# Context features projected first, expert products turned, and a routing load in eight parts

## The reference, cut to what matters

```python
# layer 0: autocorrelation attention of x with ctx, then experts
logits = x @ gate_w.T; probs = softmax(logits); vals, idx = top_k(probs, 2)   # two of 16 experts a row
w = zeros.at[rows, idx].set(vals / sum(vals))
h = silu((x @ g.T).reshape(bs, 16, 112)) * (x @ u.T).reshape(bs, 16, 112)
out = einsum('bei,hei,be->bh', h, d_r, w)
# layer 1: cross attention of the layer-normed x (text) with ctx (features)
Q = einsum('btx,dx->btd', text, Wq) + bq
K = einsum('bpx,dx->bpd', features, Wk) + bk
attn = softmax(einsum('btd,bpd->btp', Q, K) / sqrt(1024))
attended = einsum('btp,bpd->btd', attn, features)
# then x = x + tanh(g) * (...) after each part, and the quantised feed-forward
```

## Time and profile before

| | us |
|---|---|
| median of 3 runs | 1470.27 (1467.56 to 1472.78) |
| the profiled execution | 1470.33 |
| span of its trace, first to last instruction | 1468.6 |
| TensorE busy | 1265.6 (86%) |
| VectorE, ScalarE, GpSimd busy | 761.1, 549.1, 629.8 |
| mean granted TensorE clock | 0.949 of full |

### The profile page before, as it was taken

The page is one execution under the profiler, slowest core; times in us unless marked ns, Lnnn a source line. Parts: engine busy times, 40 slices in busy tenths (PEclk is TensorE's granted clock), DMA queues, the critical chain, the costliest instruction groups (busy, mean ns, idle before and its releaser), DMA issues. The chain is left out here.

```text
span 1468.6 us, 20091 instructions
## 1 busy us (share of the span) xinstructions
PE 1265.6 (86%) x5843; PEld 851.6 (58%) x5849; DVE 761.1 (52%) x1981; ACT 549.1 (37%) x936; POOL 629.8 (43%) x990
## 2 busy tenths in 40 slices
PE   3899999999966899899999994499999999838876
PEld 1444545454526844357776772388888888624443
DVE  2878888888753460013333333544345432138995
ACT  2544444444305200024444444132222222148884
POOL 4767777776540007112122123742333210047885
PEclk9999999999978599999999997699999999979999
DMA  5212124102005303127778855363233221121111
GB/s 186 87 58 63 51 84 164 38 15 101 1 0 199 149 11 103 29 69 262 257 229 257 264 194 186 88 157 115 87 114 100 89 68 34 53 65 44 57 49 80
DMA packets 53669, 156.28 MB, mean 106 GB/s; under 512 B 7152, under 2 KB 17392, under 8 KB 53488
## 3 DMA queue, kind: packets, MB, share of 16 engines
q1 hardware_dynamic: 39328, 113.65, 22.1%
q0 software_dynamic: 14288, 41.97, 10.1%
HBM read 113.09 MB, written 45.66 MB: 108 GB/s over the span
## 5 line engine op out<-in xcount | busy, mean ns | idle before, releaser
L44 PE MATMUL xa_bank<-xa_xT_hi,M_hi 128*128 128x256 f32 x512 | 154.0, 301 | 0.0
L46 PE MATMUL xa_bank<-xa_xT_hi,M_lo 128*128 128x256 f32 x512 | 145.0, 283 | 0.0
L45 PE MATMUL xa_bank<-xa_xT_lo,M_hi 128*128 128x256 f32 x512 | 144.8, 283 | 0.0
L52 PE MATMUL la_bank<-la_osum,la_tab 128*128 128x512 f32 x256 | 121.0, 617 | 15.9 <-POOL la_osum L297 14.7
L1132 PEld LDWEIGHTS ex_bank<-ex_gu,ex_xT 128*128 128x128 f32 x624 | 116.8, 190 | 21.1 <-issue 20.0
L1132 PE MATMUL ex_bank<-ex_gu,ex_xT 128*128 128x224 f32 x624 | 124.9, 353 | 0.8 <-ACT ex_xT L1057 0.8
L297 POOL TENSOR_TENSOR la_osum<-la_oprod 128x512 f32<-128x512 f32 x64 | 80.1, 1273 | 96.2 <-DVE la_oprod L476 96.2
L1325 ACT ACTIVATE xa_A<-xa_bank,shift 128x256 f32<-128x256 f32 x64 | 30.4, 475 | 210.2 <-PE xa_bank L46 210.2
L1020 POOL TENSOR_TENSOR ex_current<-ex_listed,ex_nought 128x1 int32<-128x1 int32 x42 | 8.0, 190 | 229.8 <-DVE Wq L1090 226.8
L44 PEld LDWEIGHTS xa_bank<-xa_xT_hi,M_hi 128*128 128x128 f32 x512 | 98.2, 192 | 2.8 <-issue 1.7
L45 PEld LDWEIGHTS xa_bank<-xa_xT_lo,M_hi 128*128 128x128 f32 x512 | 98.0, 191 | 2.5 <-issue 1.7
(11 more groups left out here) (274 smaller groups left out, 2872.9 us busy)
## 6 DMA issues: line engine op xcount, KB each, us to landing
produced<-Wq SPq DMA_DIRECT2D x39, 512.0 KB
ex_gu<-in_gate_up SPq DMA_DIRECT2D x16, 896.0 KB, 6.6
X<-in_x SPq DMA_DIRECT2D x8, 1024.0 KB, 7.5
la_v_raw<-in_ctx SPq DMA_DIRECT2D x16, 512.0 KB
produced<-la_zeros SPq DMA_DIRECT2D x16, 512.0 KB, 5.1
normal<-rt_xn SPq DMA_DIRECT2D x16, 512.0 KB, 3.6
xa_fT<-in_ctx_T SPq DMA_DIRECT2D x8, 1024.0 KB, 5.5
xa_f<-in_ctx SPq DMA_DIRECT2D x8, 1024.0 KB, 5.6
```

The lines of the kernel that those rows point to most:

```text
L44: pe.matmul(out, a[0], b[0], start=first, stop=False)
L45: pe.matmul(out, a[0], b[1], start=False, stop=False)
L46: return pe.matmul(out, a[1], b[0], start=False, stop=last)
L52: return pe.matmul(out, a, b, start=first, stop=last)
```

## The change

In `route` and before it: the last batch's mean and deviation are made at the start of `route` instead of at the end of `lag_attention`; the weight that is loaded early is Wq, and the second, Wk, is loaded in eight parts of 512 KB, one ahead of the loop and one after every second store. In `experts`: gate and up weights are the stationary operands and the turned rows move, 128 wide, so that both products come out turned; the transpose of `hid` and the copy `hT` are gone. In `context_attention`: M is applied to the context features (`g_block`) instead of to the text. The features are split in hi and lo, and turned text `xT` is a plain float32 copy. Scores of a batch come in one piece at its end. `M_lo` is made partly on VectorE. All batches are written out.

```diff
 lag_attention (pool; the vector engine alike)
-                if before2 and before2[2] == 1:
+                if before2 and before2[2] == 1 and not (isinstance(before2[1], int) and before2[1] == B - 1):
                     scales_after.on_pool(pool, before2[1])
 route
+            def load_part(k):
+                sp.dma_start(W[1][:, k, :], Wk[k * P:(k + 1) * P, :]).then_inc(s["wk_in"], 16)
+            load_part(0)
             for t in range(TILES):
-                if t == TILES // 2:
-                    sp.dma_start(W[1][:], Wq.rearrange("(k p) n -> p k n", p=P)).then_inc(s["wq_in"], 16)
                 sp.wait_ge(s["xn_ready"], t + 1)
                 sp.dma_start(normal[t * P:(t + 1) * P, :], xn[:, t % RING, :]).then_inc(stored[t % RING], 16)
+                if t % 2 == 1 and t // 2 + 1 < KD:
+                    load_part(t // 2 + 1)
...
+            norm.prepare(pool)
+            norm.on_pool(pool, B - 1, 0)
             pool.wait_ge(s["no_list"], 16)
...
+                if t == TILES - 2:
+                    act.wait_ge(norm.ready, 1)
                 act.activation(xn[:, t % RING, :], X[:, t, :], ACT.Identity, ...
...
+            norm.variance(dve, X, B - 1, 0)
             dve.memset(key_bias[:, :, 3].bitcast(F32), 0.0)
 experts, scalar
-                act.wait_ge(s["gu_done"], g + 1)
-                act.activation(sg, bank[0][:, 0:INTER], ACT.Silu).then_inc(s["silu_done"], 1)
+                act.wait_ge(s["gate_done"], g + 1)
+                act.activation(sg[:], bank[0][0:INTER, 0:P], ACT.Silu).then_inc(s["silu_done"], 1)
                 rows_out(g + 1)
-                act.wait_ge(s["h_turned"], g + 1)
-                act.activation(hT, bank[1][0:INTER, 0:P], ACT.Copy).then_inc(s["hT_ready"], 1)
 experts, vector
-                dve.tensor_tensor(hid[:], sg, bank[0][:, INTER:UP_COLS], ALU.mult).then_inc(s["hid_done"], 1)
+                dve.wait_ge(s["up_done"], g + 1)
+                dve.tensor_tensor(hT[:], sg[:], bank[1][0:INTER, 0:P], ALU.mult).then_inc(s["hT_ready"], 1)
 experts, tensor
-                        m = pe.matmul(bank[0][:, 0:UP_COLS], xT[:, k, :], gu[:, slot, k * UP_COLS:(k + 1) * UP_COLS], start=(k == 0), stop=(k == KD - 1))
+                    for half, done in enumerate(("gate_done", "up_done")):
+                        for k in range(KD):
+                            at = k * UP_COLS + half * INTER
+                            m = pe.matmul(bank[half][0:INTER, 0:P], gu[:, slot, at:at + INTER], xT[:, k, :], start=(k == 0), stop=(k == KD - 1))
+                        m.then_inc(s[done], 1)
                     turn(g + 1)
-                    pe.wait_ge(s["hid_done"], g + 1)
-                    pe.transpose(bank[1][0:INTER, 0:P], hid[:], ident[:]).then_inc(s["h_turned"], 1)
                     pe.wait_ge(s["hT_ready"], g + 1)
 context_attention, sync
+            def load_turned(b):
+                at_least(sp, s["g_pe"], KD * b)
+                sp.dma_start(fT[:], ...
 scalar, ahead of the batches
+            for m in range(3):
+                merged_high(m)
+            (the two gates' Tanh)
+            merged_high(3)
+            features_high(0)
+            for m in range(4, KD):
+                merged_high(m)
...
+            row_high(0)
+            for m in range(KD):
+                if m == 6:
+                    normalise(0)
+                g_out(0, m)
+            rows_out(0)
+            features_high(1)
 pool, ahead of the batches
+            gather(0, 2)
+            gather(0, 3)
+            for m in range(POOL_LOW, KD):        # POOL_LOW = 5
+                merged_low(pool, m).then_inc(s["m_lo_pool"], 1)
+            gather(1, 0); gather(1, 1); norm.on_pool(pool, 0); gather(1, 2); gather(1, 3)
 vector, ahead of the batches
+            for m in range(3):
+                merged_low(dve, m).then_inc(s["m_lo"], 1)
+            combine(0, 0)
+            merged_low(dve, 3).then_inc(s["m_lo"], 1)
+            features_low(0)
+            combine(0, 1)
+            merged_low(dve, 4).then_inc(s["m_lo"], 1)
+            combine(0, 2)
+            combine(0, 3)
+            row_low(0)
 tensor
+            def row_term(b):
+                pe.wait_ge(s["fT_lo"], 4 * b + 4)
...
+            def scores(b):
+                pe.wait_ge(s["xT_act"], 2 * b + 2)
+                pe.wait_ge(s["xT_dve"], 2 * b + 2)
+                pe.wait_ge(s["g_out"], KD * (b + 1))
...
+            row_term(0)
+            for m in range(KD):
+                g_block(0, m)
+            turn(0)
+            scores(0)
+            for b in range(B):
+                if b + 1 < B:
+                    row_term(b + 1)
+                    g_block(b + 1, 0)
+                    g_block(b + 1, 1)
+                turn_shares(b)
+                if b + 1 < B:
+                    for m in range(2, KD):
+                        g_block(b + 1, m)
+                    turn(b + 1)
+                outputs(b)
+                if b + 1 < B:
+                    scores(b + 1)
```

More of the change, by code:

```diff
@@ new lines, in row_high, with g_out, normalise @@
+            def row_high(b):
+                act.wait_ge(s["row_pe"], b + 1)
+                at_least(act, s["s_pe"], b)
+                act.activation(row[0][:], row_bank, ACT.Identity, bias=half_constant).then_inc(s["row_hi"], 1)
+            def g_out(b, m):
+                act.wait_ge(s["g_pe"], KD * b + m + 1)
+                at_least(act, s["s_pe"], b)
+                act.activation(G[:, m, :], bank[2 + m % 2][:, 0:L], ACT.Identity, bias=shift[:, m:m + 1]).then_inc(s["g_out"], 1)
+            def normalise(b):
+                act.wait_ge(norm.ready, b + 1)
+                at_least(act, s["turned"], 2 * b)
+                at_least(act, s["p_turned"], b)
+                at_least(act, s["gains"], 3 * b)
+                for j in range(2):
+                    tile = 2 * b + j
+                    act.activation(xn[:, j, :], X[:, tile, :], ACT.Identity, scale=norm.scale[:, tile:tile + 1],
+                                   bias=norm.shift[:, tile:tile + 1]).then_inc(s["xn_ready"], 1)
@@ new lines, in _ @@
+            combine(1, 1)
+            rows_out(0)
+            combine(1, 2)
+            combine(1, 3)
+            features_low(1)
+            for b in range(B):
+                dve.wait_ge(s["s_pe"], b + 1)
+                for j in range(2):
+                    last = dve.tensor_reduce(row_max[:, j:j + 1], bank[4 + j][:, 0:L], AX_X, ALU.max)
+                last.then_inc(s["chain"], 1)
+                dve.wait_ge(s["chain"], b + 1)
+                dve.tensor_scalar(bias, row_max, -SCORE_SCALE, None, ALU.mult).then_inc(s["maxed"], 2)
+                if b + 1 < B:
+                    row_low(b + 1)
+                dve.wait_ge(s["exped"], 2 * b + 2)
+                dve.tensor_reduce(row_sum, prob, AX_X, ALU.add).then_inc(s["gains"], 1)
+                dve.wait_ge(s["gains"], 3 * b + 1)
+                dve.reciprocal(row_sum, row_sum).then_inc(s["gains"], 1)
+                dve.wait_ge(s["gains"], 3 * b + 2)
+                dve.tensor_scalar(row_gain, row_sum, tg, None, ALU.mult).then_inc(s["gains"], 1)
+                if b + 1 < B:
@@ L1417, in step @@
-                if two:
-                    combine(b + 2, 1)
-                if before:
-                    dve.wait_ge(s["added"], 4 * b)
-                    after.variance(dve, X, b - 1)
-                if two:
-                    combine(b + 2, 2)
-                if two:
-                    combine(b + 2, 3)
-                if more:
-                    rows_low(b + 1)
-            batches(dve, step)
+                        combine(b + 2, i)
+                if b + 1 < B:
+                    rows_out(b + 1)
@@ new lines, in _ @@
+                dve.wait_ge(s["gains"], 3 * b + 3)
+                for i in range(4):
+                    j, h = i // 2, i % 2
+                    dve.wait_ge(s["out_pe"], 4 * b + i + 1)
+                    x = X[:, 2 * b + j, h * 512:(h + 1) * 512]
+                    dve.scalar_tensor_tensor(out=x, in0=bank[out_bank[i]][:], scalar=row_gain[:, j:j + 1], in1=x,
+                                             op0=ALU.mult, op1=ALU.add).then_inc(s["added"], 1)
+                if b + 2 < B:
+                    features_low(b + 2)
@@ L1430, in _ @@
+                dve.wait_ge(s["added"], 4 * b + 4)
+                after.variance(dve, X, b)
         @block.tensor
```

368 lines of the change are left out of this document (149 added, 219 removed).

## The result

The changed kernel takes 1424.06 us (median of 4 runs, 1422.62 to 1431.22) against 1470.7 of the kernel before beside it: 0.9694 of it, with a 95% interval of 0.9657 to 0.9731. The forecast was 1418.8 with a range of 1404 to 1438. It is faster, inside the range, by 46.6 us instead of 51.5.

What follows compares the result with a forecast made beforehand. TensorE bounds the context batches and expert loop; elsewhere GpSimd's scale chain, a store stall with low clock, and a late context start cost time. 1470.3 - 6.2 - 18.9 - 5.1 - 21.3 = 1418.8 us, range 1404 to 1438.

Steps and rivals of the forecast that it cites:

- Part 1: End of the lag stage: last scales moved to the start of routing, where other waits cover them; -6.2 us.
- Part 2: Routing loop up to the `column_sum` copy: Wk in eight parts removes ScalarE's store stall and the clock's fall; -18.9 us.
- From the copy at 481.43, three turns of the loop follow: Routing loop's end: three turns at 2.29 us, then two without transposes, 3.6 us, so the loop ends at 492.4.
- the first block of M is ... 7.3: Behind the routing loop: 16 products of 512 columns at 0.457 us, 7.3 instead of 8.62 at a clock not yet risen.
- A clock of 0.50 in the loop: Sign listed as proving the forecast wrong: TensorE at clock 0.50 in the routing loop, where about 0.95 was expected.
- Rival A: Routing loop: full queues stall again and the clock falls to 0.50, giving back 18.9 us, 1437.7; chance 0.10.
- Rival C: Routing loop: the clock stays low throughout, half its instructions being transposes; 35.5 us more, 1454; chance 0.05.
- Part 3: 39 expert tiles: turned gate and up products start 0.110 us apart, a tile takes 6.25 us, 0.13 less; -5.1 us.
- rival E: Better than forecast: expert product spacing near 0.10 us, or late stores of `y` no longer costing; 1400 to 1408; chance 0.04.
- Rival D: Expert tiles: loads at 0.190 us set the turned products' pace, +94.8 us instead of -5.1, 1518.7; chance 0.04.
- Part 4: Context attention's start: first product at 917.1 instead of 943.47, -26.4 us, with 5.1 given back; -21.3 us.
- Rival B: Context batches: scores wait for copies and VectorE's additions, 1 to 2 us in seven batches, 1426 to 1433; chance 0.11.

Runs made afterwards that it cites:

- the second pair: The changed kernel and the kernel before, both unedited, run and traced again later on another chip: 1414.24 us against 1461.64, ratio 0.9686.
- the first pair: The first traces of the changed kernel and the kernel before, laid side by side; measured 1424.06 us against 1470.7, ratio 0.9694.

## Why the prediction was right, and where its terms were off

**Part 1** held: -5.7 measured. Routing's first instruction is issued 1.8 us after the start of VectorE's last addition instead of 8.7, which is 6.9 less. Of that 0.8 comes back because the router's weight lands 3.1 us after its issue instead of 2.2, and 0.3 is a lag stage that ended that much later. Both covers (VectorE's under the router's weight, GpSimd's under 14 tiles) were there.

**Part 2** had the right mechanism and was 4.6 us too large (3.7 in the second pair). Two steps failed. "From the copy at 481.43, three turns of the loop follow" is four: VectorE's copy of tile 11 stands at the end of turn 9, and turns 10 to 13 follow; in the trace after it is 9.17 us from 475.90 to 485.07, that is 4 x 2.29. And "the first block of M is ... 7.3" took the full clock. From the `logit` copy to the `column_sum` copy it is 10.7 us, forecast 8.4, because the clock was at 0.50 from 487.4 to 494.2. I looked only for idle time as what lowers the clock; here TensorE is busy, but 16 columns wide. "A clock of 0.50 in the loop" was on my list of what would make the forecast wrong, and for the loop's last 2 us it came.

Rival A (the ring starves) didn't come, though it was near: the queues were full at 390 GB/s, where I had reckoned 327 with a little to spare. Rival C didn't come either: 1.00 in 456 to 478. The Trainium skill ("TensorE: Matmul & The Clock Gate", "Part 4: PE-mode transpose") has transposes as not engaging the full clock. The trace after does not agree: from 448.83 to 452.5 TensorE has only transposes, the clock rises between 452 and 454, and it stays at 1.00 with a third of the recorded instructions transposes. (The prediction says half; that is so by operations, eight transposes and eight products a tile, but a product is two instructions.)

**Part 3** had the spacing right (0.109 for 0.110) and two errors that nearly cancel, which is luck. The undisturbed tile was priced too long: 6.09 to 6.17 us where I had 6.25, against 6.36 before. The loop with small weight loads shows what 38 undisturbed periods take, 232.6 us, and 38 x 6.36 is 241.7, so they alone give 9.1. And late stores were a term that I did not price: they cost 10.4 us in the first trace after (242.9 - 232.6) and 4.0 before (245.7 - 241.7), so 2.8 were left. Over all traces the loop gained 4.4, near the forecast of 5.1. I had named late stores in rival E, as something that might cease; they grew. That a shorter tile leaves the queue less time for the same bytes fits the three lengths of tile: 2 to 4 us of late stores at 6.36, 5 to 12 at 6.1, 14 to 17 at 5.8.

Rival D is refuted: the spacing is 0.109 where the loads are recorded at 177 ns. The Trainium skill's rule (same page, "Part 3: Packing small matmuls") that a load overlaps only with products of another row group would give the longer one; the trace does not agree here either.

**Part 4** held best. The first product was forecast 15.0 us after the stage's start and came at 15.4, and the batches gave back 4.5 of the 5.1 forecast. The outputs of the last batch, not in my sum, took 7.13 instead of 8.66 in the first pair, but that is no gain of the change: the clock happened to fall behind them and not among them. In the second trace of the same kernel it fell again:

```profile
1217.69 8.83 PE L1524 MATMUL xa_bank<-xa_f,xa_pT 128*128 128x512 f32 x16 [0.69 <-ACT xa_pT L1358]
```

The 15 us had a second bound close behind the one that I costed, the wait for `ones`; I followed VectorE's queue and never asked what else TensorE waits for. Rival B (waits in the batches) didn't come: TensorE is busy 329.7 of 330.6 us there.

The time came out 5.3 us above the forecast's 1418.8, and the gain 5.5 short in the traces: by 4.6 (part 2), 2.4 (part 3) and 0.5 (part 1), less 1.9 that the context stage and the feed-forward gave more. In the second pair it is 3.6 short, all of it part 2. The inner range of 1408 to 1430 does not follow from its own terms, which give 1412 to 1434; the result lies in both.

## What to carry to other kernels

When a step gets shorter, ask first what has to be moved during it: the loop's own transfers had 4% less time, and in the first trace 6.3 of the 9.1 us gained went into waits for them, until a second buffer took the wait off the engine that feeds the critical one. A large load issued in one piece among small stores costs the stall and then the clock; parts between the stores cost neither. And a serial chain may be shortened only down to the next wait of the same engine: list all its waits at that place before pricing the removal of one.

## What the hardware showed that was not expected

The granted clock fell to 0.50 while TensorE was recorded busy throughout, among 4.6 us of products with 16 columns each; one eighth of a 512-column block per tile among them delayed and shortened the fall. And a loop that holds the full clock need not get it back: behind the stall the same loop stayed at 0.50 for 23.9 us of busy TensorE before and for 18 us with Wk in one load, up to the wide products of M.

A VectorE addition of 128 x 1024 float32 in SBUF took 8.9 us instead of 1.28 while GpSimd made three subtractions in SBUF, and the next one, in the same row, took 1.28 again. Of the 8.9, 7.2 are covered by the subtractions. In the kernel before, an addition that met one subtraction of 2.35 took 3.8. So the addition took about its own time and the subtractions' together, and the subtractions took no longer than before (2.4). It was off the path here.

```profile
897.66 10.28 DVE L1381 SCALAR_TENSOR_TENSOR X<-ffn_row,weights,X 128x1024 f32<-128x1024 f32 x2 [0.74 <-DMA ffn_row<-produced,xa_small_u]
```

```profile
898.36 7.10 POOL L1220 TENSOR_TENSOR M_lo<-M,M_hi 128x1024 fp32r<-128x1024 f32 x3
```

An instruction of a float32 product with 64 moving columns is hardly cheaper than with 128 (0.098 against 0.109 us from start to start). And the first traces of both kernels had 8 us of TensorE pauses that none of the twelve later ones has.
